# Output projection per 112 tokens instead of 224, and the exponential of the softmax per head with its sum, in an attention-and-FFN layer on eight cores

## The chip, the cores and the metric

The kernel runs on the 8 NeuronCores of one Trainium2 chip. Each core computes one half of the sequence of one of the four batches; the cores exchange nothing. The metric is the device time of the slowest core, in microseconds (us). All arithmetic is float32.

## The reference

Input x is (4, 4096, 1024). It is normalised (`xn`), and the output is x plus two branches of xn: a windowed attention and a gated FFN.

```python
xn = _layernorm(x, axis=-1)                     # eps 1e-5
x = x + attn(xn, wq, wk, wv, wo, ...) + ffn(xn, W_r, W_k, W_v, mu_r, mu_k)

def attn(x, ...):                               # 16 heads of 64, 4 KV heads
    q = rmsnorm((x @ wq.T).reshape(B, L, 16, 64)); k = rmsnorm(...4 heads...); v = ...
    bias = slopes * rel, and -inf where (rel > 0) | (rel < -16)
    p = softmax(q @ k / 8 + bias)
    return (p @ v).reshape(B, L, 1024) @ wo.T

def ffn(x, W_r, W_k, W_v, mu_r, mu_k):
    xr = mu_r * x + (1 - mu_r) * x_prev; xk = mu_k * x + (1 - mu_k) * x_prev
    return sigmoid(xr @ W_r.T) * (square(relu(xk @ W_k.T)) @ W_v.T)
```

Since a query sees only itself and the 16 tokens before it, 112 queries need 128 keys.

## The kernel before, in words

A core has 2048 tokens and 16 tokens of halo before them. It works on them in four tiles of 512 tokens (`NT`, loop over `tt`); features lie on the partitions in 8 chunks of 128 (`NCH`), tokens along the free axis. The weights are loaded again for every tile, in halves, into three slots of `wslot`.

One tile goes through these stages, all in the order in which the code writes them, for every engine has its own recorded queue (`T`, `V`, `S`, `G`, `SY` for TensorE, VectorE, ScalarE, GpSimd and SyncE) that is replayed at the end. Every instruction is replayed by line 176, so line numbers don't tell the stages apart in the profile; the names of the tiles do.

1. Statistics of the layer norm (line 373 on): matmuls against `invD` give sums in `psA`, `psB` and `psPV`; VectorE works them up on one partition in the rows `r0`, `r1`, `r2` of `lrow` (products, difference, plus epsilon, reciprocal), ScalarE takes the square root into `r3`, and matmuls spread the rows over the partitions. TensorE has nothing else to do meanwhile. Then `xnbuf` is made.
2. K and V projections, then the Q projection, into `kbuf`, `vbuf` and `qbuf`.
3. The RMS norms of q and k, with two output blocks of the FFN's first matmul (`emit_r_filler`) between them.
4. The attention, in five subtiles of 112, 112, 112, 112 and 64 queries (`SUBTILES`), called subtile 0 to 4 here.
5. The three matmuls of the FFN (`ffn_phase`), which read `xmix`, `scr` and `xmix`.

The attention is what the change touches. For subtile ss it emits:
- `emit_qk`: 16 matmuls (one for each head) into the four banks of `psS`;
- `emit_softmax`: VectorE scales and adds the mask `logm` into `pbuf`; ScalarE takes the exponential of all 16 heads in one instruction of 16 x 128 columns; VectorE adds up each head (TENSOR_REDUCE into `lbuf`), takes the reciprocal and multiplies;
- for the subtile before: `emit_pv`, 16 matmuls into `psPV`, and ScalarE's copy of them into `asub`. `asub` holds two subtiles side by side (2 x 112 columns for each of 8 chunks), and after every second one `emit_oproj` multiplies all 224 columns by `wo`: 8 output blocks of 8 matmuls, by turns into `psA` and `psB`, each block taken out by VectorE, which adds x and writes `xnbuf`. So it follows `emit_pv` of subtile 1 and of subtile 3;
- `emit_transposes`: 16 transposes of `pbuf` into `psS`, and ScalarE's copies into `ptbuf`.

After the loop come `emit_pv` and `emit_oproj` for subtile 4 alone, with 64 columns. A float32 matmul or weight load stands as two records in the profile (x16 is 8 matmuls); a transpose is one.

The queues are in order: on TensorE the transposes of a subtile, which wait for its softmax, stand behind whatever of the subtile before is emitted there; on ScalarE the copy into `asub` stands behind the exponential of the next subtile.

Of the kernel before, what the change touches and what calls it, by code (L numbers as in the profile page):

```python
# [7 lines left out]
AF = mybir.ActivationFunctionType  # L8
ALU = mybir.AluOpType
AX = mybir.AxisListType  # L10

D = 1024
NCH = 8
NH = 16
# [4 lines left out]
HALO = 16  # L19
TILE = 512  # L20
NT = CORE_T // TILE
TT = TILE + HALO
# [158 lines left out]
def build_program():  # L181
# [24 lines left out]
    sb = lambda name, shape: nc.alloc_sbuf_tensor(name, shape, F32).ap()  # L206
    pm = lambda name, shape: nc.alloc_psum_tensor(name, shape, F32).ap()
    xbuf = sb("xbuf", [128, NCH * TT])
    xnbuf = sb("xnbuf", [128, NCH * TT])
# [4 lines left out]
    vbuf = sb("vbuf", [128, 5 * 256])  # L214
    pbuf = sb("pbuf", [128, NH * 128])
    ptbuf = sb("ptbuf", [128, NH * 112])
    asub = sb("asub", [128, NCH * 224])
    lbuf = sb("lbuf", [128, 2 * NH])
    rbuf2 = sb("rbuf2", [128, 2 * 512])
    qrow = sb("qrow", [NH, 2 * TILE])  # L220
    krow = sb("krow", [NKV, 2 * TT])
    lrow = sb("lrow", [1, 3 * TT])
    wslot = sb("wslot", [128, 3 * 4096])
    ident = sb("ident", [128, 128])
    logm = sb("logm", [112, NH * 128])
# [17 lines left out]
    with nc.Block() as block:  # L243
# [5 lines left out]
        s_v = _Sem(nc, "s_v")  # L249
        s_s = _Sem(nc, "s_s")  # L250
        s_g = _Sem(nc, "s_g")

        T = _EngRec("tensor")
        V = _EngRec("vector")
        S = _EngRec("scalar")
# [4 lines left out]
        C_EPSLN = lambda p: scal[0:p, 1:2]  # L260
        C_EPSRM = lambda p: scal[0:p, 2:3]
        C_NEG1 = lambda p: scal[0:p, 3:4]
        C_ONE = lambda p: scal[0:p, 4:5]
# [68 lines left out]
        try:  # L332
          for tt in range(NT):
# [33 lines left out]
            for ci in range(NCH):  # L367
# [5 lines left out]
            r0 = lrow[0:1, 0:TT]  # L373
            r1 = lrow[0:1, TT:2 * TT]
            r2 = lrow[0:1, 2 * TT:3 * TT]
            r3 = r1
            V.wait_ge(s_t.h, STATS_T)
            V.tensor_copy(lrow[0:1, 0:512], psA[0:1, 0:512])
            V.tensor_copy(lrow[0:1, 512:TT], psPV[0:1, 0:16])
# [3 lines left out]
            bank_free["B"] = (s_v.h, s_v.n)  # L383
            psPV_rows_done = (s_v.h, s_v.n)
            V.tensor_tensor(r2, r0, r0, op=ALU.mult)
            V.tensor_tensor(r1, r1, r2, op=ALU.subtract)
            V.tensor_scalar_add(r1, r1, C_EPSLN(1))
            s_v.inc(V.reciprocal(r2, r1))
            S.wait_ge(s_v.h, s_v.n)
            s_s.inc(S.activation(r3, r2, AF.Sqrt))  # L390
# [2 lines left out]
                                           op0=ALU.mult, op1=ALU.mult))  # L393
# [29 lines left out]
            for ko in range(2):  # L423
                for (c0, c1) in [(0, 512), (512, TT)]:
                    bank = "A" if (nb % 2 == 0) else "B"
                    nb += 1
                    ps = psA if bank == "A" else psB
                    mm_gate(bank)
                    for ci in range(NCH):
                        T.wait_ge(s_v.h, xn_chunk_v[ci])  # L430
                        lhs = wkv_v[:, 512 * ci + 128 * ko: 512 * ci + 128 * ko + 128]
                        last = T.matmul(ps[0:128, 0:c1 - c0], lhs,
                                        xnbuf[:, TT * ci + c0: TT * ci + c1],
                                        start=(ci == 0), stop=(ci == NCH - 1))
# [5 lines left out]
            for g, (goff, glen) in enumerate(VGROUPS):  # L440
                bank = "A" if (g % 2 == 0) else "B"
                ps = psA if bank == "A" else psB
                mm_gate(bank)
                for ci in range(NCH):
                    lhs = xnbuf[:, TT * ci + goff: TT * ci + goff + glen]
                    last = T.matmul(ps[0:glen, 0:256], lhs,
                                    wkv_v[:, 512 * ci + 256: 512 * ci + 512],
                                    start=(ci == 0), stop=(ci == NCH - 1))
# [11 lines left out]
            for half in range(2):  # L460
# [3 lines left out]
                for co in range(4 * half, 4 * half + 4):  # L464
                    bank = "A" if (co % 2 == 0) else "B"
                    ps = psA if bank == "A" else psB
                    mm_gate(bank)
                    for ci in range(NCH):
                        lhs = wq_v[:, 512 * ci + 128 * (co % 4):
                                   512 * ci + 128 * (co % 4) + 128]  # L470
                        last = T.matmul(ps[0:128, 0:512], lhs,
                                        xnbuf[:, TT * ci + HALO: TT * ci + TT],
                                        start=(ci == 0), stop=(ci == NCH - 1))
# [19 lines left out]
            for ci in range(NCH):  # L493
                last = V.scalar_tensor_tensor(
                    xmix[:, 512 * ci: 512 * ci + 512],
                    xmix[:, 512 * ci: 512 * ci + 512], mur[:, ci:ci + 1],
                    xnbuf[:, TT * ci + HALO - 1: TT * ci + TT - 1],
                    op0=ALU.mult, op1=ALU.add)
# [5 lines left out]
            for ci in range(NCH):  # L504
# [4 lines left out]
                    op0=ALU.mult, op1=ALU.add)  # L509
# [78 lines left out]
            for ci in range(NCH):  # L588
# [3 lines left out]
                else:  # L592
                    T.wait_ge(psS_free[0], psS_free[1])
                    ps = psS[:, 0:512]
# [55 lines left out]
            def emit_softmax(msk, qk_t, qlen, kw):  # L650
                V.wait_ge(s_t.h, qk_t)
                sin = psS[0:qlen, 0:NH * 128].rearrange(
                    "q (h k) -> q h k", h=NH)[:, :, 0:kw]
                min_ = msk[0:qlen, 0:NH * kw].rearrange("q (h k) -> q h k", h=NH)
                pout = pbuf[0:qlen, 0:NH * kw].rearrange("q (h k) -> q h k", h=NH)
                s_v.inc(V.scalar_tensor_tensor(pout, sin, C_SCALE(qlen), min_,
                                               op0=ALU.mult, op1=ALU.add))
                S.wait_ge(s_v.h, s_v.n)
                s_s.inc(S.activation(pbuf[0:qlen, 0:NH * kw],
                                     pbuf[0:qlen, 0:NH * kw], AF.Exp))  # L660
                V.wait_ge(s_s.h, s_s.n)
                s_v.inc(V.tensor_reduce(lbuf[0:qlen, 0:NH], pout, axis=AX.X,
                                        op=ALU.add))
                s_v.inc(V.reciprocal(lbuf[0:qlen, NH:2 * NH], lbuf[0:qlen, 0:NH]))
                rb = lbuf[0:qlen, NH:2 * NH].unsqueeze(-1).broadcast_to(
                    [qlen, NH, kw])
                s_v.inc(V.tensor_tensor(pout, pout, rb, op=ALU.mult))
                return s_v.n
# [20 lines left out]
                        psS[0:kw, 512 * b: 512 * b + per_bank * qlen]))  # L689
                ptbuf_evac_s = s_s.n  # L690

            def emit_pv(ss, qoff, qlen, kw, ptevac):
                nonlocal pv_evac_v
                T.wait_ge(s_s.h, ptevac)
                if pv_evac_v is not None:
                    T.wait_ge(s_s.h, pv_evac_v)
                else:
                    T.wait_ge(psPV_free[0], psPV_free[1])
                for s in range(NH):
                    h = 2 * (s % 8) + s // 8  # L700
                    kv = h % 4
                    lhs = vbuf[0:kw, 256 * ss + 64 * kv: 256 * ss + 64 * kv + 64]
                    rhs = ptbuf[0:kw, qlen * s: qlen * s + qlen]
                    pp = 64 * (h % 2)
                    col = 128 * (h // 2)
                    last = T.matmul(psPV[pp:pp + 64, col: col + qlen], lhs, rhs,
                                    start=True, stop=True)
                s_t.inc(last)
                S.wait_ge(s_t.h, s_t.n)
                pvin = psPV[:, 0:1024].rearrange("p (c t) -> p c t", t=128)[:, :, 0:qlen]  # L710
                po = 112 * (ss % 2)
                aout = asub[:, 0:NCH * 224].rearrange(
                    "p (c t) -> p c t", t=224)[:, :, po:po + qlen]
                s_s.inc(S.copy(aout, pvin))
                pv_evac_v = s_s.n

            def emit_oproj(qoff0, nq):
                T.wait_ge(s_ws[wo_info[0][0] % 3].h, wo_info[0][1])
                T.wait_ge(s_ws[wo_info[1][0] % 3].h, wo_info[1][1])
                T.wait_ge(s_s.h, pv_evac_v)  # L720
                for co in range(NCH):
                    wo_v = wslot_view(wo_info[0][0] if co < 4 else wo_info[1][0])
                    bank = "A" if (co % 2 == 0) else "B"
                    ps = psA if bank == "A" else psB
                    mm_gate(bank)
                    for ci in range(NCH):
                        lhs = wo_v[:, 512 * ci + 128 * (co % 4):
                                   512 * ci + 128 * (co % 4) + 128]
                        last = T.matmul(ps[0:128, 0:nq], lhs,
                                        asub[:, 224 * ci: 224 * ci + nq],  # L730
                                        start=(ci == 0), stop=(ci == NCH - 1))
                    s_t.inc(last)
                    V.wait_ge(s_t.h, s_t.n)
                    xsl = xbuf[:, TT * co + HALO + qoff0: TT * co + HALO + qoff0 + nq]
                    ysl = xnbuf[:, TT * co + HALO + qoff0: TT * co + HALO + qoff0 + nq]
                    s_v.inc(V.scalar_tensor_tensor(ysl, ps[0:128, 0:nq], C_ONE(128),
                                                   xsl, op0=ALU.mult, op1=ALU.add))
                    bank_free[bank] = (s_v.h, s_v.n)

            for ss, (qoff, qlen) in enumerate(SUBTILES):  # L740
                kw = qlen + 16
                msk, qk_t = emit_qk(ss, qoff, qlen, kw)
                pnorm_v = emit_softmax(msk, qk_t, qlen, kw)
                if prev is not None:
                    emit_pv(*prev)
                    pss, pqoff, pqlen = prev[0], prev[1], prev[2]
                    if pss % 2 == 1:
                        emit_oproj(pqoff - 112, 224)
                emit_transposes(pnorm_v, qlen, kw)
                prev = (ss, qoff, qlen, kw, ptbuf_evac_s)  # L750
            emit_pv(*prev)
            emit_oproj(prev[1], prev[2])
            YADDS_V = s_v.n
            PSS_GATE = (s_s.h, ptbuf_evac_s)
            PSPV_GATE = (s_s.h, pv_evac_v)
# [168 lines left out]
```

## Time and profile before

| | us |
|---|---|
| median of 2 runs | 2076.78 (2060.93 and 2092.64) |
| the profiled execution, its own time | 2061.27 |
| its span on the slowest core (core 3) | 2059.8 |
| spans of the other cores | 2027.4 to 2055.8 |
| PE busy in that span | 1795.1 (87%) |
| DVE busy | 486.0 (24%) |
| ACT busy | 192.0 (9%) |
| POOL busy | 53.2 (3%) |

The profile is of one execution, core 3; times in its rows are from the start of the span. PE is TensorE's matmuls, PEld its weight loads, DVE VectorE, ACT ScalarE, POOL GpSimd, SP SyncE. "PEclk" is the clock granted to TensorE as a share of 2.4 GHz.

### The profile page before, as it was taken

How to read it: one execution, taken by the hardware profiler on the slowest of the kernel's cores; microseconds unless marked ns; L12 is line 12 of the kernel's file. 1: busy time of each engine (PE TensorE's matmuls, PEld its weight loads, DVE VectorE, ACT ScalarE, POOL GpSimd, SP SyncE). 2: the span in 40 equal slices, each digit the busy share in tenths (PEclk: the TensorE clock that was granted, in tenths of full speed). 3: DMA queues.
4: the chain of work that ended last, by engine and by line, in shares of the span. 5: the costliest groups of instructions: out<-in, count | busy, mean ns of one | idle time of the engine just before them, and what ended most of it. 6: DMA issues, size and time to landing. Idle time of an engine off the chain costs nothing.

```text
span 2059.8 us, 15116 instructions; the slowest of 8 cores (2027.4 to 2059.8 us)
## 1 busy us (share of the span) xinstructions
PE 1795.1 (87%) x6240; PEld 1081.9 (53%) x6240; DVE 486.0 (24%) x546; ACT 192.0 (9%) x260; POOL 53.2 (3%) x36
## 2 busy tenths in 40 slices
PE   2798698999979869899988986899997996889998
PEld 0442488744344249874435426795442633878443
DVE  0344222000133422200023343310104423320010
ACT  0001211000000121100000002100000001110000
POOL 0000000000200000000020000000011000000001
PEclk9898677699989867779998976878998996787999
DMA  7021000322122100032230210003223120001311
GB/s 210 1 82 41 1 1 0 113 93 82 58 65 82 41 0 1 0 124 82 82 123 6 77 41 1 1 1 124 82 82 122 41 82 1 1 1 45 119 41 41
DMA packets 59835, 112.67 MB, mean 55 GB/s; under 512 B 1860, under 2 KB 10312, under 8 KB 59544
## 3 DMA queue, kind: packets, MB, share of 16 engines
q1 hardware_dynamic: 59768, 111.70, 16.6%
q8 instruction: 52, 0.85, 0.2%
q14 instruction: 15, 0.12, 0.0%
HBM read 103.31 MB, written 8.39 MB: 54 GB/s over the span
## 4 chain that ended last, share of the span: by engine, by line
PE 83%; DVE 8%; ACT 4%; issue 2%; DVEq 1%; DMA 1%; SPq 1%; POOL 0%; ACTq 0%; POOLq 0%
PE psA L176 38%; PE psB L176 34%; PE psS L176 9%; DVE pbuf L176 3%; PE psPV L176 2%; DVE lbuf L176 1%; DVE lrow L176 1%; DVE xnbuf L176 1%; ACT pbuf L176 1%; DVEq L176 1%; DMA xbuf<-xin 1%; ACT ptbuf L176 1%; SPq L176 1%; ACT L176 1%; ACT asub L176 0%
## 5 line engine op out<-in xcount | busy, mean ns | idle before, releaser
L176 PE MATMUL psA<-xmix,wslot 128*128 128x512 f32 x512 | 246.9, 639 | 10.1 <-ACT xmix L176 7.8
L176 PE MATMUL psB<-xmix,wslot 128*128 128x512 f32 x512 | 229.4, 602 | 2.0 <-DVE qrow L176 2.0
L176 PE MATMUL psA<-xnbuf,wslot 128*128 128x512 f32 x384 | 181.7, 623 | 13.1 <-DVE xnbuf L176 10.4
L176 PE MATMUL psA<-asub,wslot 128*128 128x224 f32 (+1 forms) x768 | 169.1, 390 | 13.9 <-ACT asub L176 13.9
L176 PEld LDWEIGHTS psA<-xmix,wslot 128*128 128x128 f32 x512 | 104.3, 206 | 143.2 <-issue 143.2
L176 PEld LDWEIGHTS psA<-asub,wslot 128*128 128x128 f32 x768 | 159.3, 246 | 17.3 <-issue 15.9
L176 PE MATMUL psB<-asub,wslot 128*128 128x224 f32 (+1 forms) x768 | 168.1, 388 | 0.0
L176 PEld LDWEIGHTS psB<-xmix,wslot 128*128 128x128 f32 x512 | 98.3, 193 | 128.7 <-issue 128.7
L176 PEld LDWEIGHTS psB<-asub,wslot 128*128 128x128 f32 x768 | 159.9, 246 | 1.4
L176 PEld LDWEIGHTS psA<-xnbuf,wslot 128*128 128x128 f32 x384 | 74.0, 198 | 111.2 <-issue 111.1
L176 PE MATMUL psS<-ident,pbuf 112*128 112x112 f32 (+1 forms) x320 | 50.6, 336 | 90.4 <-DVE pbuf L176 90.4
L176 PE MATMUL psB<-xnbuf,wslot 128*128 128x512 f32 (+1 forms) x384 | 127.3, 480 | 0.0
L176 PE MATMUL psB<-scr,wslot 128*128 128x512 f32 x256 | 112.5, 592 | 0.0
L176 PE MATMUL psA<-scr,wslot 128*128 128x512 f32 x256 | 112.5, 592 | 0.0
L176 PE MATMUL psS<-kbuf,qbuf 64*112 64x128 f32 (+1 forms) x640 | 97.7, 355 | 12.6 <-ACT ptbuf L176 12.6
L176 POOL TENSOR_TENSOR xnbuf<-xnbuf,pbuf 128x512 f32<-128x512 f32 x32 | 53.0, 1655 | 1998.9 <-DVE pbuf L176 1998.9
L176 PEld LDWEIGHTS psS<-kbuf,qbuf 64*112 64x112 f32 (+1 forms) x640 | 92.9, 242 | 20.4 <-issue 20.4
L176 PEld LDWEIGHTS psB<-xnbuf,wslot 128*128 128x128 f32 x384 | 64.2, 191 | 65.1 <-issue 65.1
L176 PEld LDWEIGHTS psS<-ident,pbuf 112*128 112x128 f32 (+1 forms) x320 | 45.8, 189 | 94.1 <-issue 93.9
L176 ACT ACT_TABLE_LOAD x24 | 30.8, 1283 | 637.3 <-DVE lrow L176 296.0
L176 DVE SCALAR_TENSOR_TENSOR pbuf<-psS,scal,logm 112x2048 f32<-112x2048 f32 (+1 forms) x19 | 41.4, 2180 | 183.6 <-PE psS L176 183.6
L176 PE MATMUL psPV<-ptbuf,vbuf 128*64 128x112 f32 (+1 forms) x640 | 80.5, 324 | 3.8 <-ACT ptbuf L176 3.8
(85 smaller groups left out, 1167.4 us busy)
## 6 DMA issues: line engine op xcount, KB each, us to landing
wslot<-w_wq SPq DMA_DIRECT2D x8, 2048.0 KB, 14.4
wslot<-w_wo SPq DMA_DIRECT2D x8, 2048.0 KB, 9.2
wslot<-w_wr SPq DMA_DIRECT2D x8, 2048.0 KB, 10.1
wslot<-w_wkf SPq DMA_DIRECT2D x8, 2048.0 KB, 13.1
wslot<-w_wvf SPq DMA_DIRECT2D x8, 2048.0 KB, 12.7
xbuf<-xin SPq DMA_DIRECT2D x4, 2112.0 KB, 19.3
yout<-xnbuf SPq DMA_DIRECT2D x4, 2048.0 KB, 9.3
wslot<-w_wk SPq DMA_DIRECT2D x4, 1024.0 KB, 12.6
```

Source lines behind the costliest of these rows:

```text
L176: inst = getattr(eng, attr)(*a, **kw)
```

## The change

Three edits.

1. `asub` holds one subtile, and `emit_pv` and `emit_oproj` are one function, `emit_pv_oproj`: the output projection is done for each subtile by itself, 112 columns wide for four of them, 64 for the last.
2. The exponential is 16 instructions, one for each head, and each also gives the sum of its row (`accum_out`) into `lbuf`. The TENSOR_REDUCE is gone.
3. In the statistics, `r1 + eps - r2` is one instruction instead of two, and `r3` has a row of its own in `lrow`.

```diff
-    asub = sb("asub", [128, NCH * 224])
+    asub = sb("asub", [128, NCH * 112])
...
-            V.tensor_tensor(r1, r1, r2, op=ALU.subtract)
-            V.tensor_scalar_add(r1, r1, C_EPSLN(1))
+            V.scalar_tensor_tensor(r1, r1, C_EPSLN(1), r2,
+                                   op0=ALU.add, op1=ALU.subtract)
...
-                s_s.inc(S.activation(pbuf[0:qlen, 0:NH * kw],
-                                     pbuf[0:qlen, 0:NH * kw], AF.Exp))
+                for hh in range(NH):
+                    last = S.activation(pbuf[0:qlen, kw * hh: kw * hh + kw],
+                                        pbuf[0:qlen, kw * hh: kw * hh + kw],
+                                        AF.Exp,
+                                        accum_out=lbuf[0:qlen, hh:hh + 1])
+                s_s.inc(last)
                 V.wait_ge(s_s.h, s_s.n)
-                s_v.inc(V.tensor_reduce(lbuf[0:qlen, 0:NH], pout, axis=AX.X,
-                                        op=ALU.add))
...
-            def emit_pv(ss, qoff, qlen, kw, ptevac):
+            def emit_pv_oproj(ss, qoff, qlen, kw, ptevac):
...
-            def emit_oproj(qoff0, nq):
...
-                        last = T.matmul(ps[0:128, 0:nq], lhs,
-                                        asub[:, 224 * ci: 224 * ci + nq],
+                        last = T.matmul(ps[0:128, 0:qlen], lhs,
+                                        asub[:, 112 * ci: 112 * ci + qlen],
                                         start=(ci == 0), stop=(ci == NCH - 1))
...
                 if prev is not None:
-                    emit_pv(*prev)
-                    pss, pqoff, pqlen = prev[0], prev[1], prev[2]
-                    if pss % 2 == 1:
-                        emit_oproj(pqoff - 112, 224)
+                    emit_pv_oproj(*prev)
                 emit_transposes(pnorm_v, qlen, kw)
                 prev = (ss, qoff, qlen, kw, ptbuf_evac_s)
-            emit_pv(*prev)
-            emit_oproj(prev[1], prev[2])
+            emit_pv_oproj(*prev)
```

On TensorE, in the first tile, from the last two output blocks of the first projection on, before (`psA` and `psB` from `asub` are blocks of the projection, `psS` from `ident` the transposes, `psS` from `kbuf` the QK matmuls, `psPV` the PV matmuls):

```order
L176 MATMUL psA<-asub,wslot 128x224 x8
L176 MATMUL psB<-asub,wslot 128x224 x8
L176 MATMUL psS<-ident,pbuf 128x112 x16
L176 MATMUL psS<-kbuf,qbuf 112x128 x16
L176 MATMUL psPV<-ptbuf,vbuf 64x112 x16
L176 MATMUL psS<-ident,pbuf 128x112 x16
```

and from the same place of the changed kernel:

```order
L176 MATMUL psA<-asub,wslot 128x112 x8
L176 MATMUL psB<-asub,wslot 128x112 x8
L176 MATMUL psS<-ident,pbuf 128x112 x16
L176 MATMUL psS<-kbuf,qbuf 112x128 x16
L176 MATMUL psPV<-ptbuf,vbuf 64x112 x16
L176 MATMUL psA<-asub,wslot 128x112 x8
```

Behind every PV there is now a projection of half the columns, 64 matmuls, where before there was one behind every second. Per tile that makes 4 x 64 matmuls of 112 columns instead of 2 x 64 of 224; the 64 matmuls of 64 columns stay.

On ScalarE, from the exponential of subtile 1 to the copy behind that of subtile 2, before (`ptbuf` from `psS` are the copies of the transposes):

```order
L176 ACTIVATE pbuf<-pbuf 112x2048
L176 COPY asub<-psPV 128x8x112
L176 COPY ptbuf<-psS 128x448 x4
L176 ACTIVATE pbuf<-pbuf 112x2048
L176 COPY asub<-psPV 128x8x112
```

and in the changed kernel:

```order
L176 ACTIVATE pbuf,lbuf<-pbuf 112x128 x16
L176 COPY asub<-psPV 128x896
L176 COPY ptbuf<-psS 128x448 x4
L176 ACTIVATE pbuf,lbuf<-pbuf 112x128 x16
L176 COPY asub<-psPV 128x896
```

The order is the same; sixteen instructions now stand ahead of each copy into `asub`.

## Rows read from the trace of the kernel before

**Rows 1.** The page: busy time, share of the span, instructions, of each engine.
```profile
PE 1795.1 (87%) x6240; PEld 1081.9 (53%) x6240; DVE 486.0 (24%) x546; ACT 192.0 (9%) x260; POOL 53.2 (3%) x36
```

**Rows 2.** The page: the chain that ended last, by engine.
```profile
PE 83%; DVE 8%; ACT 4%; issue 2%; DVEq 1%; DMA 1%; SPq 1%; POOL 0%; ACTq 0%; POOLq 0%
```

**Rows 3.** Waits: who waited for whom, total us, times, longest us.
```profile
PE psS L176 <- DVE pbuf L176: 90.4, 12, 11.1
...
PE psS L176 <- DVE lrow L176: 41.7, 4, 10.7
...
PE psA L176 <- ACT asub L176: 13.9, 12, 1.3
```

**Rows 4.** Timeline of PE, third tile's attention: start, us, records [idle before <-releaser].
```profile
1272.35 3.22 PE L176 MATMUL psS<-ident,pbuf 112*128 112x112 f32 x16 [4.82 <-DVE pbuf L176]
1276.34 6.42 PE L176 MATMUL psS<-kbuf,qbuf 64*112 64x128 f32 x32 [0.77 <-ACT ptbuf L176]
1282.69 5.21 PE L176 MATMUL psPV<-ptbuf,vbuf 128*64 128x112 f32 x32
1289.15 3.27 PE L176 MATMUL psA<-asub,wslot 128*128 128x224 f32 x16 [1.25 <-ACT asub L176]
...
1313.44 1.70 PE L176 MATMUL psS<-ident,pbuf 112*128 112x112 f32 x16
1316.07 3.38 PE L176 MATMUL psS<-kbuf,qbuf 64*112 64x128 f32 x32 [0.93 <-ACT ptbuf L176]
1319.37 2.95 PE L176 MATMUL psPV<-ptbuf,vbuf 128*64 128x112 f32 x32
1329.29 3.22 PE L176 MATMUL psS<-ident,pbuf 112*128 112x112 f32 x16 [6.97 <-DVE pbuf L176]
...
1337.23 5.25 PE L176 MATMUL psPV<-ptbuf,vbuf 128*64 128x112 f32 x32
...
1368.11 1.09 PE L176 MATMUL psS<-ident,pbuf 64*80 64x64 f32 x16
```

**Rows 5.** Windows: us, busy time and records of each engine, PEclk, DMA share, GB/s.
```profile
1278.00:1282.00 4.00, 4.00 (x24) 4.00 (x24) 0.00 (x0) 0.00 (x0) 0.00 (x0) 0.50 0.00 0
1289.20:1313.40 24.20, 24.20 (x128) 24.19 (x129) 6.25 (x10) 0.00 (x0) 0.00 (x0) 1.00 0.00 1
1374.00:1400.00 26.00, 26.00 (x124) 26.00 (x123) 1.99 (x7) 0.00 (x0) 0.00 (x0) 0.50 0.00 1
605.20:606.80 1.60, 1.60 (x17) 1.60 (x15) 0.00 (x0) 0.59 (x1) 0.00 (x0) 1.00 0.00 0
275.00:297.00 22.00, 22.00 (x97) 21.31 (x97) 2.71 (x6) 0.00 (x0) 0.00 (x0) 0.81 0.00 1
```

**Rows 6.** Timeline of ACT, subtile 2 of the third tile.
```profile
1285.40 1.91 ACT L176 ACTIVATE pbuf<-pbuf 112x2048 f32<-112x2048 f32 x1 [9.21 <-DVE pbuf L176]
1287.99 0.91 ACT L176 COPY asub<-psPV 128x896 f32<-128x896 f32 x1 [0.68 <-PE psPV L176]
1314.08 1.84 ACT L176 COPY ptbuf<-psS 128x448 f32<-128x448 f32 x4 [25.18 <-PE psS L176]
```

**Rows 7.** Groups by form: busy us, mean ns of one, idle before.
```profile
L176 ACT COPY ptbuf<-psS 128x448 f32<-128x448 f32 x64 | 33.0, 535 | 185.8 <-PE psS L176 185.8
...
L176 ACT ACTIVATE pbuf<-pbuf 64x1280 f32<-64x1280 f32 x4 | 5.1, 1272 | 24.0 <-DVE pbuf L176 24.0
...
L176 ACT COPY kbuf<-psB 128x16 f32<-128x16 f32 x8 | 1.4, 173 | 8.8 <-PE psB L176 8.8
```

**Rows 8.** Groups by form: the DVE operations of the softmax and of the statistics.
```profile
L176 DVE TENSOR_REDUCE lbuf<-pbuf 112x16 f32<-112x2048 f32 x16 | 36.6, 2286 | 40.0 <-ACT pbuf L176 40.0
...
L176 DVE TENSOR_TENSOR lrow<-lrow 1x528 f32<-1x528 f32 x8 | 5.6, 696 | 0.7
...
L176 DVE SCALAR_TENSOR_TENSOR lrow<-lrow,scal 1x528 f32<-1x528 f32 x4 | 3.0, 756 | 8.7 <-ACT lrow L176 8.7
...
L176 DVE TENSOR_SCALAR lrow<-lrow,scal 1x528 f32<-1x528 f32 x4 | 1.9, 482 | 0.3
```

More of the change, by code:

```diff
@@ L221, in build_program @@
     krow = sb("krow", [NKV, 2 * TT])
-    lrow = sb("lrow", [1, 3 * TT])
+    lrow = sb("lrow", [1, 4 * TT])
     wslot = sb("wslot", [128, 3 * 4096])
@@ L375, in build_program @@
             r2 = lrow[0:1, 2 * TT:3 * TT]
-            r3 = r1
+            r3 = lrow[0:1, 3 * TT:4 * TT]
             V.wait_ge(s_t.h, STATS_T)
@@ L710, in emit_pv @@
                 pvin = psPV[:, 0:1024].rearrange("p (c t) -> p c t", t=128)[:, :, 0:qlen]
-                po = 112 * (ss % 2)
-                aout = asub[:, 0:NCH * 224].rearrange(
-                    "p (c t) -> p c t", t=224)[:, :, po:po + qlen]
+                aout = asub[:, 0:NCH * 112].rearrange(
+                    "p (c t) -> p c t", t=112)[:, :, 0:qlen]
                 s_s.inc(S.copy(aout, pvin))
                 pv_evac_v = s_s.n
-            def emit_oproj(qoff0, nq):
                 T.wait_ge(s_ws[wo_info[0][0] % 3].h, wo_info[0][1])
@@ L733, in emit_oproj @@
                     V.wait_ge(s_t.h, s_t.n)
-                    xsl = xbuf[:, TT * co + HALO + qoff0: TT * co + HALO + qoff0 + nq]
-                    ysl = xnbuf[:, TT * co + HALO + qoff0: TT * co + HALO + qoff0 + nq]
-                    s_v.inc(V.scalar_tensor_tensor(ysl, ps[0:128, 0:nq], C_ONE(128),
+                    xsl = xbuf[:, TT * co + HALO + qoff: TT * co + HALO + qoff + qlen]
+                    ysl = xnbuf[:, TT * co + HALO + qoff: TT * co + HALO + qoff + qlen]
+                    s_v.inc(V.scalar_tensor_tensor(ysl, ps[0:128, 0:qlen], C_ONE(128),
                                                    xsl, op0=ALU.mult, op1=ALU.add))
```

## The prediction

> **What bounds the kernel now.** The busy times come first: TensorE is busy for 1795.1 of 2059.8 us and no other engine reaches a quarter [rows 1]; 83% of the chain of waits is its work [rows 2]. So a change is worth what it does to TensorE's own work and to its idle time. The waits, read next, say where it idles: 90.4 us before the transposes, for the softmax on DVE; 41.7 us for the rows of the statistics; 13.9 us for ScalarE's copy into `asub` [rows 3]. The change works on all three. The timeline of PE then gives the attention stage in sequence, and I take the third tile as the pattern. Three things are to be seen in it [rows 4]:
> - Subtiles 1 and 3 have nothing but PV behind which to hide their softmax, and TensorE idles 4.82 and 6.97 us. Subtiles 2 and 4 have the projection of 224 columns there and no idle time before their transposes (1313.44, 1368.11).
> - After each such gap the same work takes about twice as long: 16 transposes 3.22 us against 1.70, QK 6.42 against 3.38.
> - Subtile 0's wait stands ahead of these rows; it is the longest of its kind, 11.1 us [rows 3], and has no cover, before or after the change.
>
> The windows show why: the granted clock is 0.50 (1.2 GHz) in QK of subtile 2, behind the gap, and 1.00 (2.4 GHz) in the projection that follows [rows 5].
>
> **How long a matmul of 112 columns takes** is the main question. A record of the 224-column form takes 24.2/128 = 0.189 us at clock 1.00 and about 0.23 us at 0.81 [rows 5]. By its columns alone the 112-column form would take half, and the edit would be free. But the 64-column form, in 1374 to 1400, takes 26.0/122 = 0.213 us at clock 0.50, with PEld busy for all of the 26 us: there the weight loads, 128 columns each, set the pace, not the moving columns. A form of 16 columns, at clock 1.00, also shows PEld busy all the time, at about 1.60/15 = 0.107 us [rows 5], half of 0.213. So a record that loads 128 columns of weights doesn't go below 0.107 us at 2.4 GHz and 0.213 us at 1.2 GHz, and 112 columns lie below that floor: 0.189/2 = 0.094. A projection of one subtile is 128 records: 128 x 0.107 = 13.7 us at 2.4 GHz, 27.3 us at 1.2 GHz, where the half of a 224-column one cost 12.1.
>
> The Trainium skill ("TensorE: Matmul & The Clock Gate", LDWEIGHTS) gives a weight load as its columns divided by 1.2, which is 107 ns for 128 columns, and ties it to no clock. The row at clock 1.00 agrees; the row at 0.50, 0.213 us, doesn't. By the page alone a cold projection would cost no more than a warm one, and the slow rival below would not exist.
>
> **The exponential.** One of 2048 columns takes 1.91 us [rows 6], one of 1280 takes 1.27 [rows 7]: 0.833 ns a column and 0.205 us fixed. So 128 columns take 0.312 us and 80 take 0.272. What handing out a sum costs no row shows. Low end: four copies of 448 columns issued back to back take 1.84 us where one alone takes 0.535 [rows 6, 7], so neighbours overlap by 0.10 us, and 16 take 16 x 0.312 - 15 x 0.10 = 3.5 us. High end: each sum costs as much as the smallest ScalarE operation, 0.173 us [rows 7], and nothing overlaps: 16 x 0.485 = 7.8 us. I take no overlap and no extra, 16 x 0.312 = 5.0 us, since it is the row's own duration and lies between; for 80 columns 16 x 0.272 = 4.4.
>
> The Trainium skill ("ScalarE: Activation LUTs", What ACT_TABLE_LOAD costs) has 186 ns + 0.833 ns a column and an overlap of about 93 ns between neighbours. That would make 3.3 us of the 16, an estimate from the page alone, and the sum below about 4 x 8 us smaller; the fixed part in this trace is 0.205 us instead.
>
> **The sum, for one tile at clock 1.00.** The stages between the subtiles are of two kinds.
>
> From QK's end to the next transposes. Before [rows 4]: subtile 2, 1282.69 to 1313.44, 30.75; subtile 3, 1319.37 to 1329.29, 9.9, and subtile 1, which has the same work, as much; subtile 4, 1337.23 to 1368.11, 30.9. Together 81.5. After, each of them is the same: QK ends, DVE masks, the exponentials run, and only then can ScalarE copy into `asub`. In subtile 2 now the exponential starts 2.7 us after QK's end [rows 4, 6]; 5.0 of it, 0.09 to the copy, 0.91 for it and 0.25 until the projection starts make 8.9 us; PV (5.2 us cold, 3.0 warm) is inside. For subtile 4 mask and exponentials are shorter: about 7.5. So PE idles before each projection, some 6 us with a warm PV, where it idled 1.25. A gap of 4.82 was enough to take the clock to 1.2 GHz [rows 4], so each projection starts cold. Rows show how long a cold start lasts: the PV of 32 records took 5.21 instead of 2.95 us, so it got its clock after 2 x 2.26 = 4.5 us. I take 4 us at half speed, a loss of 2.0. The projection thus takes 13.7 + 2.0 = 15.7. VectorE normalises meanwhile, so the transposes follow at once. After: 3 x 8.9 + 7.5 + 4 x 15.7 = 97.0, which is +15.5 us.
>
> From those transposes to QK's end. Before: 10.3 for subtile 2 (1272.35 to 1282.69), 5.9 for subtile 3 (1313.44 to 1319.37), 7.9 for subtile 4 (1329.29 to 1337.23). After, the projection ahead of them has the clock up, so subtile 2 takes 5.9 too, and subtile 4 about 4.7 (1.70, 0.93 and a QK of 80 instead of 128 columns, 32 x 0.107 x 80/128): -4.4 and -3.2, -7.6 us. Subtile 1 stays, it comes after subtile 0's bare wait.
>
> Subtile 0: its wait is the whole softmax chain. It loses the reduce, 2.29 + 0.09 [rows 8], and the exponential goes from 1.91 to 5.0: +0.7 us.
>
> Subtile 4's own PV and 64-column projection: unchanged, 0.
>
> Statistics: a TENSOR_TENSOR of 0.70 and a TENSOR_SCALAR of 0.48 with 0.08 between become one of 0.76 [rows 8]. TensorE waits for this chain, so it counts: -0.5 us. The row of its own for `r3` orders nothing anew: 0.
>
> The DMAs that follow the projections (second half of `W_r`, next x) are issued behind the same last instruction as before; the single `asub` costs no wait, since PV of the next subtile stands behind the projection on TensorE anyway. VectorE takes out twice as many blocks, 112 columns each, in the shadow of the next block. All 0.
>
> One tile: +15.5 - 7.6 + 0.7 - 0.5 = +8.1; four: +32. At clock 0.81, which core 3 has in part of its first two tiles [rows 5], the floor is 0.131, and 4 x 16.8 against 2 x 29.4 adds 2 us more a tile; I leave it in the range. On the profiled execution, 2061.3 us, that makes 2093 us. The median of the two runs, 2076.78, lies 15.5 us higher, halfway to a run of 2092.64; I count from the profiled one. So +1.6%, under the 2% that a measurement of this kernel can tell from no change.
>
> **Rivals.**
> 1. The sums are dear (slower). ScalarE spends 0.34 us or more on each head. Each us more in the exponentials comes 5 times a tile on the path (subtiles 0 to 4, all wait for it), 20 in all: at 5.5 us, 0.34 each, the change passes +2%; at the high end of 7.8 it makes 2093 + 20 x 2.8 = 2149 us. For it: no row shows an accumulating activation, and the small ones have a large fixed part. Against: nothing shows an extra at all.
> 2. The projection of 112 columns never gets the clock up (slower). The 64-column form stayed at 0.50 for all its 27 us [rows 5]. If 112 do so too, each projection costs 27.3 instead of 15.7, and the transposes and QK behind them are cold: 4 x 11.6 + 7.6 = +54 a tile, 2309 us. Against: PV of subtile 2, which also moves 112 columns a record, did get its clock back, after 4.5 us [rows 4].
> 3. Neighbouring exponentials overlap (no change). At 3.5 us each block is 1.5 shorter: 2093 - 20 x 1.5 = 2063 us.
> 4. The stall was worth more (faster). The 64-column projection is cold only because the clock falls just ahead of it, in short pieces of work and waits (1368.11 on). If the new rhythm leaves it at 2.4 GHz it costs 13.7 instead of 27.3: with rival 3 as well, 2063 - 4 x 13.6 = 2009 us; in half of the tiles 2036.
>
> **How the numbers follow.** The forecast (4.2 to 5.5 us for 16 exponentials) 0.41; rival 1 0.33; rival 2 0.05; rival 3 0.13; rival 4 0.08. Slower by over 2% is rival 1 past its point and rival 2, 0.38; faster by over 2% only rival 4 in full, 0.07; within 2%, 0.55. The range leaves out rival 2 and the depth of rival 4: from 2045 us (overlap, with the clock held in a tile or so) to 2149 us (the high end of the sums). The predicted time is 2093 us.
>
> **What would show it.** The exponentials: one ACTIVATE `pbuf` near 0.31 us, and 5.0 from the first of a subtile to the end of the last. PE before `psA<-asub` waits for ACT `asub` some 6 us, 16 times, where it was 13.9 us in all; the wait for DVE `pbuf` before the transposes falls from 90.4 to the 4 x 11.8 us of subtile 0. A block of 16 records of the 112-column form lasts 1.7 us at clock 1.00 and 3.4 at 0.50, with the cold part some 4 us at the head of each projection. QK of subtile 2 takes 3.4 us instead of 6.4. I am wrong on the matmuls if a warm 112-column block takes 1.5 us or less, or if the clock stays at 0.50 through a projection; wrong on ScalarE if the 16 take under 4.2 or over 5.5 us; and wrong on the place if time is gained or lost outside the attention and the statistics.

## The result, and the profile after

| | us |
|---|---|
| after, median of 27 runs (lowest) | 2118.9 (2085.3) |
| before, median of 26 runs beside them (lowest) | 2091.9 (2052.8) |
| ratio after to before, 95% interval | 1.0156, 1.0111 to 1.0200 |
| profiled execution after: span of core 3, of core 0 | 2112.1, 2078.3 |
| the same before | 2059.8, 2029.2 |

The change makes the kernel slower by 1.6% (1.1 to 2.0): more than the measurement is uncertain, and whether it reaches 2% is open. The forecast was +1.6%.

The time of the slowest core also depends on how long its die is held at a lower clock such as 0.81, which differs from run to run and from chip to chip: the ratio leaves out the runs that this slowed, the medians above take them in. For single terms I therefore use the length of the attention stage, from the last matmuls on `krow` to the FFN's first matmul behind the projections: the median over the 32 stages (8 cores, 4 tiles) of one profiled execution. It is 173.0 us before and 184.0 after. From one chip to another it moves by some 0.6 us: e3_stats_only below, whose attention is that of the kernel before, has 173.6.

The page of the changed kernel, busy time and the chain by engine, which answer to [rows 1, 2]:

```profile
PE 1832.1 (87%) x7264; PEld 1110.1 (53%) x7264; DVE 456.0 (22%) x586; ACT 246.3 (12%) x880; POOL 53.2 (3%) x36
...
PE 81%; ACT 8%; DVE 6%; issue 2%; DMA 1%; DVEq 1%; SPq 1%; ACTq 0%; POOL 0%; POOLq 0%
```

DVE lost 30 us of work and ACT gained 54; ACT's share of the chain doubled. 1024 matmul records more make PE only 37 us busier. The waits of PE (us in total, times, longest), against [rows 3]:

```profile
PE psA L176 <- ACT asub L176: 76.7, 20, 5.6
PE psS L176 <- DVE pbuf L176: 46.1, 4, 11.5
...
PE psS L176 <- DVE lrow L176: 39.3, 4, 9.9
```

The wait for the softmax lost 44 us; only subtile 0's four are left. The wait for ScalarE's copy gained 63. One wait has taken the other's place, with 18.5 us more. The third tile in the timeline of PE, from the steps of subtiles 1, 2 and 4, against [rows 4]:

```profile
1253.89 5.01 PE L176 MATMUL psPV<-ptbuf,vbuf 128*64 128x112 f32 x32
1262.44 3.73 PE L176 MATMUL psA<-asub,wslot 128*128 128x112 f32 x16 [3.54 <-ACT asub L176]
1265.95 3.14 PE L176 MATMUL psB<-asub,wslot 128*128 128x112 f32 x16
1268.92 1.95 PE L176 MATMUL psA<-asub,wslot 128*128 128x112 f32 x16
...
1279.64 1.70 PE L176 MATMUL psS<-ident,pbuf 112*128 112x112 f32 x16
1282.27 3.38 PE L176 MATMUL psS<-kbuf,qbuf 64*112 64x128 f32 x32 [0.93 <-ACT ptbuf L176]
1285.58 2.95 PE L176 MATMUL psPV<-ptbuf,vbuf 128*64 128x112 f32 x32
1294.12 3.73 PE L176 MATMUL psA<-asub,wslot 128*128 128x112 f32 x16 [5.59 <-ACT asub L176]
1297.65 2.67 PE L176 MATMUL psB<-asub,wslot 128*128 128x112 f32 x16
1300.16 1.95 PE L176 MATMUL psA<-asub,wslot 128*128 128x112 f32 x16
...
1346.59 2.95 PE L176 MATMUL psPV<-ptbuf,vbuf 128*64 128x112 f32 x32
1353.69 3.64 PE L176 MATMUL psA<-asub,wslot 128*128 128x112 f32 x16 [4.15 <-ACT asub L176]
...
1369.77 1.09 PE L176 MATMUL psS<-ident,pbuf 64*80 64x64 f32 x16
```

The transposes (1279.64) follow the projection at once and run at 1.70 us, QK at 3.38. But each projection has a gap ahead of it, its first block takes nearly twice the time of the later ones, and its second up to 1.6 times. The windows over two such heads, over the rest of one projection and over the 64-column one (us, busy time and records of each engine, PEclk, DMA share, GB/s):

```profile
1262.50:1268.00 5.50, 5.50 (x26) 5.50 (x27) 1.97 (x2) 0.00 (x0) 0.00 (x0) 0.50 0.02 3
1294.20:1299.00 4.80, 4.80 (x23) 4.80 (x24) 1.96 (x2) 0.00 (x0) 0.00 (x0) 0.50 0.00 0
1300.20:1310.80 10.60, 10.60 (x98) 10.60 (x97) 2.00 (x6) 0.00 (x0) 0.00 (x0) 1.00 0.00 0
1375.00:1401.00 26.00, 26.00 (x124) 26.00 (x123) 1.98 (x7) 0.00 (x0) 0.00 (x0) 0.50 0.00 1
```

The heads run at 1.2 GHz and recover; the 64-column projection stays there, as before. PEld is busy all the time in all four. From 1268.92 on a block of 16 records starts every 1.79 us: 0.112 us a record.

A rival to the weight loads as the cause of this pace is a fixed cost of any float32 record. PV settles it: it too moves 112 columns a record, but loads 64 weight columns and not 128 (`128*64`). A window over the PV that starts at 1285.58, at the same clock:

```profile
1285.70:1288.30 2.60, 2.60 (x32) 2.60 (x32) 2.35 (x1) 0.01 (x1) 0.00 (x0) 1.00 0.00 0
```

That is some 0.08 us a record, under the 0.112, so the pace goes with the weight columns. One thing doesn't fit and stays open: the transposes load 128 columns as well (`112*128`), and 16 of them take 1.70 us from the first start to the last end, with one starting every 0.096 us, which is under the floor too. So the floor is shown for the matmuls that stand as two records, not for every load of 128 columns.

ScalarE, subtile 1: the first two heads, the last read-out and the copy, where [rows 6] had one row of 1.91 us:

```profile
1256.60 0.31 ACT L176 ACTIVATE pbuf<-pbuf 112x128 f32<-112x128 f32 x1 [9.21 <-DVE pbuf L176]
1256.82 0.19 ACT L176 ACTIVATION_READ_ACCUMULATOR pbuf<-pbuf 112x1 f32 x1
1256.91 0.29 ACT L176 ACTIVATE pbuf<-pbuf 112x128 f32<-112x128 f32 x1
...
1261.21 0.19 ACT L176 ACTIVATION_READ_ACCUMULATOR pbuf<-pbuf 112x1 f32 x1
1261.31 0.88 ACT L176 COPY asub<-psPV 128x896 f32<-128x896 f32 x1
```

Each sum is an instruction of its own. The copy starts 4.71 us after the first exponential, 0.294 us a head.

### The profile page after: what moved, and what is told of

Same layout as the page of the kernel before. It is cut to its first block, busy times and chain, and to the rows that moved or that the text cites. A ratio compares the mean times of both kernels' runs of the same rounds, so it can differ in the third digit from the quotient of the medians.

```text
span 2112.1 us, 17932 instructions; the slowest of 8 cores (2078.3 to 2112.1 us)
## 1 busy us (share of the span) xinstructions
PE 1832.1 (87%) x7264; PEld 1110.1 (53%) x7264; DVE 456.0 (22%) x586; ACT 246.3 (12%) x880; POOL 53.2 (3%) x36
## 4 chain that ended last, share of the span: by engine, by line
PE 81%; ACT 8%; DVE 6%; issue 2%; DMA 1%; DVEq 1%; SPq 1%; ACTq 0%; POOL 0%; POOLq 0%
PE psA L176 39%; PE psB L176 35%; PE psS L176 7%; ACT pbuf L176 4%; DVE pbuf L176 3%; DVE lrow L176 1%; DVE xnbuf L176 1%; ACT ptbuf L176 1%; DMA xbuf<-xin 1%; DVEq L176 1%; ACT L176 1%; ACT asub L176 1%; SPq L176 1%; PE psPV L176 1%; DVE kbuf L176 0%
## 5 line engine op out<-in xcount | busy, mean ns | idle before, releaser
L176 PE MATMUL psA<-asub,wslot 128*128 128x112 f32 (+1 forms) x1280 | 214.0, 338 | 76.7 <-ACT asub L176 76.7
L176 PEld LDWEIGHTS psA<-asub,wslot 128*128 128x128 f32 x1280 | 204.6, 251 | 80.2 <-issue 80.2
L176 PE MATMUL psB<-asub,wslot 128*128 128x112 f32 (+1 forms) x1280 | 197.3, 320 | 0.0
L176 PEld LDWEIGHTS psB<-asub,wslot 128*128 128x128 f32 x1280 | 191.9, 237 | 0.0
L176 ACT ACT_TABLE_LOAD x24 | 30.8, 1283 | 642.6 <-DVE lrow L176 302.0
L176 ACT ACTIVATE pbuf<-pbuf 112x128 f32<-112x128 f32 (+1 forms) x320 | 91.6, 287 | 102.7 <-DVE pbuf L176 102.7
L176 PE MATMUL psS<-kbuf,qbuf 64*112 64x128 f32 (+1 forms) x640 | 75.2, 296 | 14.1 <-ACT ptbuf L176 14.1
L176 PEld LDWEIGHTS psA<-scr,wslot 128*128 128x128 f32 x256 | 50.7, 198 | 65.3 <-issue 65.3
L176 PEld LDWEIGHTS psB<-scr,wslot 128*128 128x128 f32 x256 | 50.7, 198 | 65.3 <-issue 65.3
L176 PEld LDWEIGHTS psS<-kbuf,qbuf 64*112 64x112 f32 (+1 forms) x640 | 71.3, 191 | 20.8 <-issue 20.8
L176 PE MATMUL psS<-ident,pbuf 112*128 112x112 f32 (+1 forms) x320 | 38.3, 282 | 46.1 <-DVE pbuf L176 46.1
```

The costliest lines, as they stand in the source:

```text
L176: inst = getattr(eng, attr)(*a, **kw)
```

## The experiments

Ten kernels. The first four ran on one chip, with 7 runs of before at a median of 2089.7 us; that chip gave no ratio with an interval, so they are read by three numbers: the median time, the attention stage, and the spans of cores 0 to 3 (their median in each run, and the median of those).

| | median, us | cores 0 to 3, us | attention stage, us |
|---|---|---|---|
| before | 2089.7 | 2043.4 | 173.0 (another chip) |
| e5_two_passes (4 runs) | 2121.4 | 2079.6 | 182.4 |
| e1_split_only (6) | 2057.9 | 2023.8 | 167.7 |
| e2_exp_only (6) | 2115.1 | 2067.1 | 180.1 |
| e4_copy_on_dve (4) | 2067.0 | 2024.4 | 169.8 |

All three put the kernels in the same order, and the spans differ from before's by four times what the stages do, to within 6 us. The next four experiments ran on another chip, where before took 2034.4 us (13 runs), the last two on a third.

### The width alone: e5_two_passes

```diff
-                        emit_oproj(pqoff - 112, 224)
+                        emit_oproj(pqoff - 112, 112)
+                        emit_oproj(pqoff, 112, 112)
```

> The kernel before, where only the projection of a pair of subtiles is done as two passes of 112 columns directly behind each other, at the same place. Nothing else moves, no wait is added, so it prices the width alone. My theory (a floor set by the 128 weight columns): 256 records of about 0.112 us, the step that the changed kernel's trace shows at clock 1.00, make 28.6 us where one pass of 224 took 24.2; +4.4 us eight times, +35 us, a ratio of about 1.017. Rival (only the moving columns count): 2 x 112 = 224, +0, ratio 1.000. A second rival (112 columns let the clock fall): PEclk at 0.50 in these passes, 54.6 us each, +240 us.

Measured: median 2121.4 us, 1.015 of before's. Attention stage 182.4 us, +9.4 a tile (expected +8.8; the 0.6 between them is no more than the difference from chip to chip). On core 0, PE's timeline, the start and the end of one pair of passes, and the window over it:

```profile
802.99 2.01 PE L176 MATMUL psA<-asub,wslot 128*128 128x112 f32 x16 [1.25 <-ACT asub L176]
804.83 1.95 PE L176 MATMUL psB<-asub,wslot 128*128 128x112 f32 x16
...
829.84 1.95 PE L176 MATMUL psB<-asub,wslot 128*128 128x112 f32 x16
831.63 1.70 PE L176 MATMUL psS<-ident,pbuf 112*128 112x112 f32 x16
```

```profile
803.00:831.50 28.50, 28.50 (x255) 28.50 (x256) 7.78 (x18) 0.00 (x0) 0.00 (x0) 1.00 0.01 1
```

28.6 us for what took 24.3 in one pass, at clock 1.00, with nothing waited for. The price of the width is shown, and so is that 112 columns don't let the clock fall: both rivals fall.

### The split without the exponential's edit: e1_split_only

```diff
-                for hh in range(NH):
-                    last = S.activation(pbuf[0:qlen, kw * hh: kw * hh + kw], ... AF.Exp,
-                                        accum_out=lbuf[0:qlen, hh:hh + 1])
+                s_s.inc(S.activation(pbuf[0:qlen, 0:NH * kw],
+                                     pbuf[0:qlen, 0:NH * kw], AF.Exp))
                 V.wait_ge(s_s.h, s_s.n)
+                s_v.inc(V.tensor_reduce(lbuf[0:qlen, 0:NH], pout, axis=AX.X,
+                                        op=ALU.add))
```

(against the changed kernel; the statistics are those of before too)

> The changed kernel with the exponential of before (one instruction, then the reduce) and the statistics of before: only the projection per subtile is left. My theory: it pays the same floor as e5_two_passes, +35 us, but gets back the stalls of subtiles 1 and 3 and the cold transposes and QK behind them; against the changed kernel the copy into asub comes 2 to 2.8 us earlier in four subtiles a tile. So -40 to -70 us against the changed kernel, +10 to -18 us against before, a ratio of 0.991 to 1.005. Rival (the split is what costs, the exponential is covered by it): the ratio stays near 1.0156, that of the changed kernel.

Measured: median 2057.9 us, 0.985 of before's; attention stage 167.7, -5.3 against before and -16.3 against the changed kernel. The split alone is a gain, in spite of the floor it pays: about 21 us, a little more than the 18 that I expected at most. The ratio 0.985 says more than that, but the spans of cores 0 to 3 give 0.990. PE's timeline on core 0, second tile, shows why it is a gain: only two of four projections have a cold head.

```profile
740.98 2.01 PE L176 MATMUL psA<-asub,wslot 128*128 128x112 f32 x16 [1.25 <-ACT asub L176]
...
766.93 3.58 PE L176 MATMUL psA<-asub,wslot 128*128 128x112 f32 x16 [2.71 <-ACT asub L176]
...
794.45 3.73 PE L176 MATMUL psA<-asub,wslot 128*128 128x112 f32 x16 [2.71 <-ACT asub L176]
...
820.83 2.01 PE L176 MATMUL psA<-asub,wslot 128*128 128x112 f32 x16 [1.25 <-ACT asub L176]
```

The gaps are 1.25 and 2.71 us where the changed kernel has 3.5 to 5.6. Over all cores and tiles the clock holds after each of the 64 gaps of about 1.25, and after 21 of the 64 gaps of 2.71: this tile is the colder kind, with a stage of 169.8 us, and in others, of some 164.7 us, no projection has a cold head.

### The exponential's edit without the split: e2_exp_only

Edit 2 of the change, on the kernel before:

```diff
-                s_s.inc(S.activation(pbuf[0:qlen, 0:NH * kw], ... AF.Exp))
+                for hh in range(NH):
+                    last = S.activation(pbuf[0:qlen, kw * hh: kw * hh + kw], ... AF.Exp,
+                                        accum_out=lbuf[0:qlen, hh:hh + 1])
+                s_s.inc(last)
...
-                s_v.inc(V.tensor_reduce(lbuf[0:qlen, 0:NH], pout, axis=AX.X,
-                                        op=ALU.add))
```

> The kernel before with only the exponential per head with its sum, and no reduce. My theory: the softmax chain grows by 0.5 us (16 exponentials take 4.7 us in the changed kernel's trace instead of 1.9, the reduce of 2.3 and its step go), which shows bare in subtiles 0, 1 and 3; in subtiles 2 and 4 the projection waits 2 and 0.5 us longer for ScalarE's copy and may start at the low clock, 2 us more each. +16 to +34 us, ratio 1.008 to 1.016. Rival (removing 40 us of DVE work from the chain shortens it): faster than before, -0.4 to -1%.

Measured: median 2115.1 us, 1.012 of before's; attention stage 180.1, +7.1. On core 0 PE waits 35.5 us for ScalarE's copy, with its longest 5.6 us, where that core waited 13.9 before, and 97.9 for the softmax, which was 91.6. Taking 40 us of reduces from VectorE gave nothing, since the instructions that replace them stand on the same chain and take longer.

By themselves the two edits are -5.3 and +7.1 us a tile, +1.8 together; both at once are +11.0. The rest, 9 us, is their meeting: the split makes four projections a tile wait for ScalarE's copy instead of two, and the exponentials stand ahead of that copy. So each of the four pays the delay and a cold head. That is an argument from the timelines; e4_copy_on_dve tests it.

### Sixteen exponentials without sums: e6_exp_no_sum

```diff
-                s_s.inc(S.activation(pbuf[0:qlen, 0:NH * kw],
-                                     pbuf[0:qlen, 0:NH * kw], AF.Exp))
+                for hh in range(NH):
+                    last = S.activation(pbuf[0:qlen, kw * hh: kw * hh + kw],
+                                        pbuf[0:qlen, kw * hh: kw * hh + kw], AF.Exp)
+                s_s.inc(last)
```

> The kernel before with the exponential in 16 instructions, one for each head, but without their sums; the reduce stays. It tells apart the 16 instructions and the 16 sums. In e2_exp_only a head takes 0.294 us, of which the row of the sum's read-out stands for some 0.09. My theory: without it a head takes 0.20 us, 16 take about 3.3 us against 1.9, so the chain is 1.4 us longer than before, bare in subtiles 0, 1 and 3, and 0.7 us in subtile 2, and its projection may start cold (2 us): +5 to +7 us a tile, +20 to +28 us, ratio 1.010 to 1.014. So the sums themselves pay for the reduce that they save: with them the chain was only 0.5 us longer. Rival (the sums are what makes them slow): 16 exponentials without sums run in under 2.5 us, ratio under 1.006.

Measured: ratio 1.0093 (1.0042 to 1.0143); attention stage 177.5, +4.5, both just under what I expected. One row of ScalarE's timeline holds all sixteen:

```profile
1267.05 3.30 ACT L176 ACTIVATE pbuf<-pbuf 112x128 f32<-112x128 f32 x16 [9.20 <-DVE pbuf L176]
```

3.30 us, 0.20 a head: neighbours do overlap by 0.1 us. The rival wanted under 2.5. The sums add 1.4 us (4.71 - 3.30), and going from one instruction to sixteen added 1.4 (3.30 - 1.91).

### The copy taken from behind the exponentials: e4_copy_on_dve

```diff
+                exp_n = s_s.n
+                if prev is not None:
+                    emit_pv(*prev)
-                V.wait_ge(s_s.h, s_s.n)
+                V.wait_ge(s_s.h, exp_n)
                 s_v.inc(V.reciprocal(lbuf[0:qlen, NH:2 * NH], lbuf[0:qlen, 0:NH]))
...
-                S.wait_ge(s_t.h, s_t.n)
+                V.wait_ge(s_t.h, s_t.n)
...
-                s_s.inc(S.copy(aout, pvin))
-                pv_evac_v = s_s.n
+                s_v.inc(V.tensor_copy(aout, pvin))
+                pv_evac_v = s_v.n
```

> The changed kernel, where VectorE instead of ScalarE copies psPV into asub, emitted between the mask and the reciprocal, so that the copy no longer stands behind the 16 exponentials. My theory: the projection starts some 4 us earlier in subtiles 2 and 3 and 2 in subtiles 1 and 4, and mostly at the full clock; the third block then waits some 2.6 us for VectorE, which is still normalising. Net -9 us a tile, -36 us against the changed kernel, ratio to before about 1.008. Rival (the width alone makes the changed kernel slow, the wait before asub is only where the time shows): the ratio stays near 1.0156.

Measured: median 2067.0 us, 0.989 of before's; attention stage 169.8, -14.2 against the changed kernel. PE's waits on core 0:

```profile
PE psA L176 <- DVE xnbuf L176: 31.7, 26, 2.4
PE psA L176 <- DVE asub L176: 27.4, 20, 1.5
```

The width and the exponentials are those of the changed kernel; only who copies differs, and the loss turns into a small gain. Against e1_split_only, 167.7, the exponentials with their sums now cost 2 us a tile; with the copy behind them they cost 16.3. So the wait behind ScalarE's queue is the cause of most of the loss. 14 us came back and not the 9 that I expected: at gaps of 1.45 us each of the four 112-column projections starts at full clock, and the third block waits 2.4 us in two projections of four and at most 0.9 in nearly all of the others, where I had 2.6 for each.

### The statistics alone: e3_stats_only

```diff
-            V.tensor_tensor(r1, r1, r2, op=ALU.subtract)
-            V.tensor_scalar_add(r1, r1, C_EPSLN(1))
+            V.scalar_tensor_tensor(r1, r1, C_EPSLN(1), r2,
+                                   op0=ALU.add, op1=ALU.subtract)
```

> The kernel before with only r1 + eps - r2 as one instruction (r3 stays where it was). My theory: a TENSOR_TENSOR of 0.70 and a TENSOR_SCALAR of 0.48 with a step of 0.08 become one of 0.76 on a chain for which TensorE waits: -0.5 us a tile, -2 us, ratio 0.999; the wait of psS for DVE lrow goes from 41.7 to about 39.5 us. Rival (something covers the chain): the wait stays at 41.7, ratio 1.000.

Measured: the wait of `psS` for DVE `lrow` is 39.3 us on the slowest core, -2.4 against [rows 3], as expected. In the time nothing can be seen of it: medians of 2130.4 us beside 2132.0, with runs of both from 2080 to 2280.

### Fewer weight loads: e7_wide_last

```diff
-                po = 112 * (ss % 2)
-                aout = asub[:, 0:NCH * 224].rearrange(
-                    "p (c t) -> p c t", t=224)[:, :, po:po + qlen]
+                aout = qbuf.rearrange(
+                    "p (c t) -> p c t", t=512)[:, :, qoff:qoff + qlen]
...
-                    if pss % 2 == 1:
-                        emit_oproj(pqoff - 112, 224)
+                    if pss == 1:
+                        emit_oproj(0, 224)
...
-            emit_oproj(prev[1], prev[2])
+            emit_oproj(224, 288)
```

> The kernel before without asub: ScalarE's copy goes into the columns of qbuf that the subtile's QK has read, and the projection is one of 224 columns behind PV of subtile 1 as before, and one of 288 columns (subtiles 2, 3 and 4) at the end. The moving columns are as many as before; the loads of 128 weight columns go from 3 x 64 matmuls to 2 x 64. My theory (the floor of the weight loads is what the 64-column form pays): 128 records of 0.24 us, 30.8, in place of 24.2 + 27.3; subtile 4 loses its cover and its chain of some 7 us stands bare. Net -14 to -17 us a tile, -56 to -68 us, ratio 0.967 to 0.973. Rival (columns count, the cover counts): no saving on the matmuls but what the low clock costs in the 64-column form (13.6 us a tile are then spared too, but the bare chain takes 7 back): ratio 0.985 to 1.00.

Measured: ratio 0.9657 (0.9560 to 0.9754); attention stage 157.7, -15.3. If the floor makes narrow projections dear, a wider one must be cheap, and it is: a block of the 288-column form starts every 3.88 us, 0.243 a record at clock 1.00, 31 us for all; the 64-column projection that is gone took 27 for less than a quarter of the columns. Not all of that is the floor. On core 3 in the second tile the wide projection takes 33.4 us with its cold head, in place of 24.3 + 27.3, 18.2 less. At 0.112 us a record the 64 columns would take 14.3 us (an estimate), so some 13 of the 18.2 are the low clock that they no longer pay, and the floor is worth about 7.6, less 2.4 for the cold head. The bare chain of subtile 4 took back some 2 us and not the 7 that my theory and the rival both had, and the wide projection took 33.4 us and not 30.8: that -15.3 lies inside -14 to -17 is in part two misses that cancel.

### Each softmax covered: e8_spread and e9_filler

e8_spread, against e7_wide_last:

```diff
-                    if pss == 1:
-                        emit_oproj(0, 224)
+                    if pss >= 1:
+                        emit_oproj(0, 224, ((0, 1, 2), (3, 4, 5), (6, 7))[pss - 1])
```

> e7_wide_last, where the 8 blocks of the 224-column projection are spread: 3 behind PV of subtile 1, 3 behind that of subtile 2, 2 behind that of subtile 3, so that each softmax but the first has some of it as cover. My theory: subtile 3's idle 7 us before its transposes is filled, QK of subtile 4 and the end run at the full clock; -8 to -14 us a tile against e7_wide_last, ratio to before 0.94 to 0.955. Rival (each piece starts cold, so what the cover gives the clock takes): no gain on e7_wide_last, ratio about 0.97.

e9_filler, against e8_spread:

```diff
-            emit_r_filler(1, "A")
...
                 pnorm_v = emit_softmax(msk, qk_t, qlen, kw)
+                if ss == 0:
+                    emit_r_filler(1, "A")
```

> e8_spread, where the second block of the FFN's first matmul (emit_r_filler) stands behind QK of subtile 0 on TensorE, in the idle 11 us, instead of ahead of it; on ScalarE its sigmoid comes behind the first exponential, which costs one more table load in subtile 1. My theory: 7 to 9 us of matmuls go into idle time; QK of subtile 0 now comes at the low clock (+3) and the table load costs 1.3: -4 to -6 us a tile against e8_spread, another 1% less. Rival (the table loads and the cold QK eat it): no change against e8_spread.

Measured: e8_spread 0.9416 (0.9319 to 0.9512, two runs), attention stage about 144.5 in the tiles without the 0.81 clock; e9_filler 0.9220 (0.9156 to 0.9283, three runs), stage 135.2. Both are faster than both kernels, e9_filler by 7.8% against before. PE's timeline of e9_filler (core 7, second tile) shows the covers of subtiles 0 and 3; subtile 1 has none, and its transposes still wait 6.48 us:

```profile
665.93 6.42 PE L176 MATMUL psS<-kbuf,qbuf 64*112 64x128 f32 x32 [0.59 <-DVE kbuf L176]
672.28 9.82 PE L176 MATMUL psA<-xmix,wslot 128*128 128x512 f32 x16
683.41 1.72 PE L176 MATMUL psS<-ident,pbuf 112*128 112x112 f32 x16 [1.30 <-DVE pbuf L176]
...
743.82 3.19 PE L176 MATMUL psA<-qbuf,wslot 128*128 128x224 f32 x16
746.84 3.19 PE L176 MATMUL psB<-qbuf,wslot 128*128 128x224 f32 x16
749.87 1.70 PE L176 MATMUL psS<-ident,pbuf 112*128 112x112 f32 x16
```

Subtile 0's wait of 11.1 us is down to 1.30; the filler gave 9 us a tile and not the 4 to 6 that I expected. Between the same points of a stage (core 6 of e8_spread, first tile, beside this one) moving the block gives 6.5 us, and 2.7 more come from the transposes and QK behind it, which run mostly at full clock; I hadn't counted those.

### The exponential's edit on that schedule: e10_best_with_sums

The diff of e2_exp_only, on e9_filler.

> e9_filler with the exponential per head with its sum, and no reduce: edit 2 of the change on a schedule where a piece of projection stands behind ScalarE's copy in three subtiles of a tile. My theory (the price of that edit is the wait of the projection for ScalarE, each time there is one, not the softmax chain): the copy comes 2 us later in subtile 2 and 2.8 in subtiles 3 and 4, +0.5 us each in subtiles 0 and 1, and two more cold starts: +8 to +13 us a tile, +32 to +52 us against e9_filler, ratio to before 0.938 to 0.948. Rival (the price is the chain's 0.5 us in each subtile, since everything is covered now): +4 to +10 us, ratio 0.924 to 0.927.

Measured: median 2001.2 us on a chip where before took 2132.0; the attention stage is what compares with e9_filler: 152.9 against 135.2, +17.7 a tile. Larger than the +8 to +13 expected, and far from the rival's 1 to 2.5. One stage of each without the 0.81 clock (core 0 and core 7, second tile), 153.5 and 136.8 us from QK of subtile 0 on, splits it: 2.9 us later at each of three projections, 2.9 and 1.7 of cold head at the first and third, 0.4 in subtile 0, 2.0 in subtile 1, whose QK now runs at 1.2 GHz throughout, and some 1 elsewhere. The lateness (8.6 in all, 7.6 expected) and the two cold heads (4.6, expected 4) came close; most of the miss is subtile 1 and the 1 us elsewhere.

## Why the prediction was right

The steps, for the third tile at clock 1.00:

- **Weight-load floor.** Right in kind: at 0.107 the floor was set a little low, 0.112 us was measured, so a projection has 14.3 us of matmuls and not 13.7. e5_two_passes shows the term alone. The sentence that no record with 128 weight columns goes below 0.107 was too wide: the transposes do.
- **The exponential.** 4.7 us against 5.0, inside its bounds, but the two parts of the guess were both off and cancelled: neighbours overlap (rival 3's premise), and each sum costs a step of 0.09 us (rival 1's). Rival 1's price of 0.34 us a head wasn't reached.
- **QK's end to the next transposes.** 25.75, 25.3, 25.05 and 23.2 us for subtiles 1 to 4, 99.3 in all, against 97.0 predicted: +17.8 and not +15.5. The gaps were 8.5 and 7.1 where I had 8.9 and 7.5; the cold heads cost 1.8 to 2.9 us each, not 2.0. The 4 us of low clock were undersized: 4.9 in subtile 2, twice the loss of 2.46.
- **Transposes to QK's end.** 5.9, 5.9, 4.7: -7.6, as predicted.
- **Subtile 0** +0.5 (predicted +0.7), **statistics** -0.6 (-0.5), **last projection** 0: still at 0.50.
- **Sum.** +10.1 us against +8.1 for this tile. Over all stages the medians without the 0.81 clock are 172.9 before and 183.9 after, +11.0; with it (4 stages before, 10 after) they are 182.1 and 192.8, +10.7, so the 2 us more a tile that I left for the range at 0.81 don't show. Four tiles thus make 40 to 42 us, where the forecast had 32. By the ratio the change costs 32 us on 2061 (23 to 41): the predicted number. So the steps were right and their sum a fifth low, and that the number fits to the digit is luck.
- **Rivals.** 1 and 3 are each half true, as said under the exponential; 2 is refuted by the windows above, 4 by the 64-column projection's 0.50.

What the prediction didn't say is that the two edits have different signs. It summed them in one stage and so gave no price for either. The runs give -5.3 and +7.1, and 9 for their meeting.

## What to carry to other kernels

A matmul that moves fewer columns than its weight load takes time for costs the weight load. Here, with 128 weight columns, a record of 16 or 112 columns took 0.107 to 0.112 us at 2.4 GHz, and one of 64 or 112 columns 0.21 us at 1.2 GHz. So splitting such a matmul for overlap pays the loads twice, and merging narrow ones is the larger gain. Before work is split to fill an engine's gaps, look at which in-order queue feeds the new pieces: what stands in it ahead of each piece is paid once for each piece. Replacing one long operation on an idle engine by sixteen short ones on a queue that the bottleneck waits for wasn't a saving here, though VectorE lost 30 us of work.

## What the runs showed of the hardware

- The sum of an activation is read out by an instruction of its own, 0.187 us long, that delays the next by 0.09 us: 0.294 us a head with sums (after), 0.206 without (e6_exp_no_sum).
- A gap of 1.25 us ahead of a projection left the clock at 2.4 GHz (64 times in e1_split_only). One of 2.71 us was followed by 3.2 to 6.5 us at 1.2 GHz in 43 of 64 cases and by none in 21; in the tile shown it cost 1.6 and 3.1 us in the matmuls behind it. In e6_exp_no_sum a gap of 2.96 us (core 1, first tile) left the clock at 1.00. So a gap of that length decides nothing by itself.
- The 112-column form, paced by its weight loads, got its clock back within 3.3 to 6.5 us in the changed kernel; the 64-column form, paced by the same loads, never did in its 27 us, in any of the 32 stages of either profile, and where it began at a higher clock it fell to 0.50 within 2 us. Why the one recovers and the other doesn't, no run shows.
- PV, with 64 weight columns, stepped below the 0.112 us of the form with 128 at the same 112 moving columns, but so did the transposes, with 128 (0.096).
